# A graph-attention layer on one core: the product that turns a block's score sums, and all that follows it, one step later in the turn

## The reference

```python
Q, K, V, Eh = x @ WQ, x @ WK, x @ WV, edge_attr @ WE     # Q, K, V by node, Eh by edge
score = K[src] * Q[dst] / sqrt(16) * Eh                  # one row of 128 an edge
score = exp(clip(score.sum(-1), -5, 5))                  # one number a head
wV = segment_sum(V[src] * score, dst);  Z = segment_sum(score, dst)
h = x + wV / (Z + 1e-6)
h = batch_norm(h) * gamma + beta
out = layer_norm(x + h)
```

## Time and profile before

| | |
|---|---|
| median of 3 runs | 2183.46 us (2179.75 to 2184.55) |
| the profiled execution's own time | 2183.48 us |
| its span in the trace | 2181.4 us |
| busy: TensorE, its weight loads | 1770.9 us (81%), 1529.2 us (70%) |
| busy: VectorE | 1744.4 us (80%) |
| busy: GpSimd, ScalarE | 1617.4 us (74%), 810.4 us (37%) |
| granted TensorE clock, mean | 0.759 of full speed |

### The profile page before, as it was taken

One profiled execution on the slowest core, in us unless ns is written; L12 is line 12 of the kernel. 1 busy time (PEld: TensorE's weight loads), 2 busy tenths in 40 slices (PEclk: granted clock), 3 DMA queues, 4 the chain that ended last, 5 costly groups with the idle time before them and its releaser, 6 DMA issues.

```text
span 2181.4 us, 39840 instructions
## 1 busy us (share of the span) xinstructions
PE 1770.9 (81%) x10843; PEld 1529.2 (70%) x10843; DVE 1744.4 (80%) x3732; ACT 810.4 (37%) x1876; POOL 1617.4 (74%) x1700
## 2 busy tenths in 40 slices
PE   8878788779778878877887887877888787788886
PEld 7766677667667767766776766766676676677775
DVE  5498878878788787887887878878788788787977
ACT  2443433433333333343333333334333334333426
POOL 7577777777777777777777777777777777777745
PEclk9988867867777776686777777778777778777768
DMA  9767666656666666666665666666666566566664
GB/s 360 253 220 226 203 196 200 217 180 210 214 195 208 194 206 208 204 208 190 210 214 181 204 215 201 203 207 202 202 201 208 189 207 218 174 209 211 203 217 118
DMA packets 190911, 451.89 MB, mean 207 GB/s; under 512 B 91470, under 2 KB 99102, under 8 KB 176800
## 3 DMA queue, kind: packets, MB, share of 16 engines
q0 software_dynamic: 78960, 214.67, 32.8%
q1 hardware_dynamic: 111792, 235.81, 31.9%
HBM read 420.34 MB, written 29.98 MB: 206 GB/s over the span
## 4 chain that ended last, share of the span: by engine, by line
PE 40%; DVE 39%; issue 14%; DVEq 5%; DMA 1%; ACT 1%; POOL 0%; SPq 0%; POOLq 0%; ACTq 0%
PE agg_ps L847 11%; DVE kq L1162 8%; DVE ssum L1165 8%; PE aux_ps L860 8%; PE eh_ps L839 7%; DVE kq L1156 6%; DVE ring L1013 5%; PE agg_ps L850 4%; DVEq L1092 4%; PE qe_ps L829 3%; DVE z_live L1114 2%; PE aux_ps L743 2%; DVE z_live L1118 2%; DVE onehot L1088 2%; DVE z_live L1105 1%
## 5 line engine op out<-in xcount | busy, mean ns | idle before, releaser
L562 POOL DMA_INDIRECT ring<-kv_rows,src_t x1613 | 1529.6, 948 | 506.0 <-issue 481.9
L839 PE MATMUL eh_ps<-we_sb,ea 128*128 128x128 f32 x3322 | 616.0, 344 | 185.9 <-DVE kq L1162 180.5
L839 PEld LDWEIGHTS eh_ps<-we_sb,ea 128*128 128x128 f32 x3322 | 545.5, 248 | 204.5 <-DVE kq L1162 102.9
L847 PE MATMUL agg_ps<-onehot,ring 128*128 128x42 f32 x3322 | 530.5, 319 | 187.2 <-DVE ring L1013 187.2
L847 PEld LDWEIGHTS agg_ps<-onehot,ring 128*128 128x128 f32 x3322 | 516.3, 237 | 226.8 <-issue 191.3
L641 ACT ACTIVATE qe_ps<-sclip 128x32 f32<-128x32 f32 x416 | 83.6, 201 | 1261.6 <-DVE sclip L1167 1259.1
L1156 DVE TENSOR_TENSOR kq<-ring,qe_ps 128x512 f32<-128x512 f32 x416 | 279.7, 672 | 241.8 <-PE qe_ps L829 174.9
L1162 DVE TENSOR_TENSOR kq<-kq,eh_ps 128x512 f32<-128x512 f32 x416 | 285.7, 687 | 45.3
L635 ACT ACTIVATE ohT<-ohT,ones 126x512 bf16<-126x512 bf16 x416 | 300.2, 722 | 13.5
L1165 DVE TENSOR_REDUCE ssum<-kq 128x32 f32<-128x512 f32 x416 | 285.0, 685 | 14.3
L633 ACT ACTIVATE ohT<-rel_wide,minus_w 126x512 bf16<-126x512 bf16 x416 | 294.9, 709 | 0.0
(11 more groups left out here) (151 smaller groups left out, 1045.1 us busy)
## 6 DMA issues: line engine op xcount, KB each, us to landing
ea<-in_edgeT SPq DMA_DIRECT2D x104, 1024.0 KB
rel_wide<-rel_rows SPq DMA_DIRECT2D x104, 512.0 KB, 4.5
ring<-kv_rows,src_t POOLq DMA_INDIRECT x1613
q_win<-q_rows SPq DMA_DIRECT2D x416, 31.5 KB
kv_rows<-ring SPq DMA_DIRECT2D x24, 512.0 KB, 10.8
q_rows<-q_st SPq DMA_DIRECT2D x27, 360.0 KB
ring<-in_xT SPq DMA_DIRECT2D x12, 512.0 KB, 8.6
xq<-in_xT SPq DMA_DIRECT2D x25, 240.0 KB, 3.1
```

The costliest lines, as they stand in the source:

```text
L562: pool.indirect_dma_start(out=kv[:, s, j, :], out_offset=None, in_=kv_rows, in_offset=bass.IndirectOffsetOnAxis(ap=src_t[:, n * TILES + j: ...
L839: last = pe.matmul(eh_ps[s % 2][:, j * P:(j + 1) * P], ea[:, s % EARS, j * P:(j + 1) * P], we_sb[:, :], start=True, stop=True)
L847: pe.matmul(msg_ps[s % 2], kv[:, room_of(s), j, D:KV], onehot[:, s % 8, j, :], start=(j == 0), stop=(j == tiles_of(n) - 1))
```

## The change

`turn_z` moves from ahead of step 7 to ahead of step 8 on TensorE, in one piece, and all that hangs on it moves by one step too: `z_shift` 9 to 10 and `z_spread` 11 to 12 on ScalarE, `turn_back` 12 to 13 on TensorE, `z_reciprocal` 10 to 11 and `attend` 14 to 15 on VectorE, and with `SHIFT` 8 to 9 also `move_z`, 9 to 10. `add_x` and `measure` stay at step 15, `remainder` and `lowest` at 4 and 6, `project_q` at 1, and SyncE's loads where they were. The number of instructions is the same on each engine.

```diff
-SHIFT = 8
+SHIFT = 9
...
                     if turn != 0:
-                        if u == 9:
+                        if u == 10:
                             z_shift(t, QP)
-                        if u == 11:
+                        if u == 12:
                             z_spread(t, QP)
...
                     if turn != 0:
-                        if u == 7:
+                        if u == 8:
                             turn_z(t, t * SLOTS + LAG, QP)
-                        if u == 12:
+                        if u == 13:
                             turn_back(t, QP)
...
                     if u == SHIFT + 1:
                         move_z(t)
                     if turn != 0:
-                        if u == 10:
+                        if u == 11:
                             z_reciprocal(t, QP)
-                        if u == 14:
+                        if u == 15:
                             attend(t, t * BLK - BLK, BLK)
                         if u == 15:
                             add_x(t, t * BLK - BLK, BLK)
```

## The result

| | before | after |
|---|---|---|
| median | 2182.2 us (4 runs, 2179.75 to 2184.55) | 2220.74 us (4 runs, 2219.33 to 2231.85) |
| ratio | | 1.018, 95% interval 1.0161 to 1.0199 |
| span of the profiled execution | 2181.4 us | 2218.4 us |
| granted clock, mean | 0.759 | 0.749 |

The change makes the kernel 38.5 us slower. The range of the forecast without that rival, 2192 to 2212, is missed.

A forecast was written before the change was run, and what follows sets the result against it. Neither TensorE nor VectorE bounds alone; they take turns, with TensorE's 13.44 us path through `turn_z` mid-turn. 14.4 + 5.5 = 19.9 us on a 2181.4 us span, plus 2.1 outside: 2203 us, range 2184 to 2222 (2192 to 2212 without rivals).

The forecast's parts named there:

- that rival: The rival "the clock takes more", placed at 2218 us, chance 0.18.
- `lowest` comes out of hiding: VectorE behind step 6: `lowest` now precedes TensorE's path through `turn_z`, no longer hidden; 0.60 us in 24 turns, +14.4 us.
- `attend` ahead of `add_x`: VectorE at step 15: `add_x` now directly follows `attend` and waits for its output; 0.22 us in 25 turns, +5.5 us.
- The rule of the Trainium skill: VectorE: a semaphore between chained instructions costs nothing extra, so the `attend` term would be 0 and the sum 5.5 us lower.
- All others keep their distance to `turn_z` and cost 0: `z_shift`, `z_reciprocal`, `z_spread`, `turn_back`, `move_z`: each costs what it cost, nothing new queues behind them; 0 us.
- the loads cost 0: SyncE and GpSimd: no DMA or wait moves, and gathers don't feel one step; 0 us.
- The clock, taken as 0: TensorE's granted clock over `turn_z`: nothing seen ties its fall to the step; 0 us, bounds -17 and +17 us.
- the clock takes more: Rival: clock low ahead of `turn_z` in six more turns, TensorE late, 15 us on top; 2218 us, chance 0.18.
- turn 20: Turn before the change with the clock low well ahead of `turn_z`: VectorE's wait 8.06 us instead of 5.57.
- the bounds of 17 us either way: Clock term's limits: `turn_z` between 0.7 us better and 0.7 worse than 6.60 us, times 24; -17 and +17 us.

The follow-up runs named there:

- e1: The changed kernel with `lowest` moved from behind step 6 to behind step 7: 2206.4 us, against 2181.9 for the kernel before on that chip.
- e2: The changed kernel with `attend` back at step 14: 2213.5 us, against 2181.9 for the kernel before on that chip.
- e4: The kernel before with one unread VectorE instruction added behind step 5 in turns 1 to 24: 2211.2 us, against 2181.9 without it on that chip.
- e5: The kernel before with two unread VectorE instructions added behind step 5: 2261.3 us, against 2186.3 without them on that chip.
- e3: The changed kernel with `lowest` behind step 7 and `attend` back at step 14: 2189.6 us, against 2181.9 for the kernel before on that chip.
- e6: The kernel before with one unread VectorE instruction added behind step 7: 2195.2 us, against 2186.3 without it on that chip.

## Why the prediction was right, and where it was short

- *`lowest` comes out of hiding, +14.4 us.* Right in mechanism and size: the wait is 6.20 us on the mean of the turns without a long one, against 6.17 forecast, and e1 gave 14.4 us back.
- *`attend` ahead of `add_x`, +5.5 us.* Right in kind and somewhat large: 0.16 us a turn instead of 0.22 by the timeline, 4.0 us. The 7.2 us of e2 hold a short wait besides, so they don't size this term. The rule of the Trainium skill that was weighed against it ("VectorE: DVE Perf Modes", "The DRAIN you can't avoid") would have had 0 here; the 0.73 us between the two starts, against 0.57, differ from it again.
- *All others keep their distance to `turn_z` and cost 0; the loads cost 0.* Right: GpSimd's gathers took the same time, and behind the long wait the step with `move_z` took 8.97 us.
- *The clock, taken as 0.* This is the term that was mis-sized: 0 in the sum, 19 to 20 us in the result, which is what is left of 38.5 us behind 14.4 and about 4 to 5.5. The waits say where it lies: behind `turn_z` 26.3 us were added, 11.9 more than the 14.4 of `lowest`, and at step 3 another 7.9. The first is the rival "the clock takes more": I had six more turns like turn 20, and six more there were, but at 1.9 us each above the normal wait, since that had grown, and not 2.5, so 11 us and not 15. The second nobody had: the bounds of 17 us either way held only the time of `turn_z` itself, which grew by 4.6 us in all (from 6.65 to 6.84 us on the mean), and neither they nor the rival held TensorE's lateness at step 3. That the total still fell into the range, 1.3 us from its end, owes something to luck. My reason to leave it at 0, that nothing in the rows ties the clock's fall to the step, was the wrong question. The fall needn't be tied to the step: with `turn_z` at its old place, an instruction that lengthens a step by 0.57 us was enough (e4, and two of them in e5).
- *What stays open.* Which turns lose the clock before `turn_z`. The loss doesn't grow evenly with the turn: beyond its own work, one unread instruction lost 15 us more, two lost 48, and one behind step 12, mostly hidden, still gave seven such turns. e3, with the turn's length nearly restored, kept 7 to 8 us and scattered over 28 us from run to run. That the length of the turn decides, and not what else the unread instruction disturbs (it lengthened gathers in e6), is argued and not shown. I cannot say ahead of a run where a given turn length comes to lie.

## What to carry to other kernels

When an instruction block that one engine runs alone is moved, ask which small works of the waiting engine lie in its shadow and which fall out of it: half of the cost here was theirs or their order's, and the other half the clock's. Where the granted clock falls and rises within a repeated stretch, as here, price an edit that lengthens the stretch at more than its own time, look for what it costs at every place where an engine waits for TensorE, and measure it in several runs. And before taking a wait away, look at how far the third engine is ahead: here GpSimd was all but the bound, so that taking away more than half of the largest wait changed nothing.

## What the runs showed of the hardware that was not expected

- TensorE at 0.50 of its clock while it doesn't idle: over all of `turn_z`, 7.20 us busy in 7.20. The same 16 products took 6.30 us where 0.60 was granted.
- 1.15 us of added VectorE work a turn, in e5, cost 3.1 us a turn (75 / 24).
- In e6 a gather that starts 0.06 to 0.12 us behind the start of an unread VectorE instruction of 128x480 takes 1.35 to 1.41 us on GpSimd instead of 0.95 (13 times of 13). GpSimd's last gather starts 10 us later than before, and VectorE's waits for gathers rose from 0.6 to 16.0 us.
- The first product of step 3 waits 0.20 us for TensorE where the 4.4 us of TensorE's work before it were granted 0.82 of the clock, and 1.66 us where they took 5.8 us at 0.59.
- One chip ran the same program in 2688.2 us where the two others took 2182 and 2186.
